# A conditioned two-layer linear attention on one core: weights read by TensorE in two interleaved halves, and row factors turned on VectorE before they go to DRAM

## What is computed

```python
xn = layernorm(x) * scale + bias
q = softmax(xn @ Wq + bq, within a head)
k = softmax(masked(xn @ Wk + bk), over the rows)
v = mask * (xn @ Wv + bv)
att = einsum('bhse,bhsd->bhed', k, v);  y = einsum('bhtd,bhed->bhte', q, att)
h = layernorm(y) * (1 + film_scale) + film_shift
x = x + silu(h) @ W_out + b_out
```

## Time and profile before

| | before |
|---|---|
| median of 3 launches (lowest to highest) | 915.3 us (910.02 to 915.97) |
| the profiled launch, its own time | 911.22 us |
| its span in the profile | 908.9 us |
| TensorE busy | 885.0 us (97%) |
| VectorE, ScalarE, GpSimd busy | 613.2, 398.4, 285.5 us |
| chain that ended last: TensorE, VectorE, DMA | 91%, 4%, 2% of the span |
| chain, rows of L419 on `psum_w` and `psum_k` | 54% and 20% |
| granted TensorE clock, mean | 0.998 |

### The profile page before, as it was taken

One profiled execution on the slowest core, in us unless ns is written; L12 is line 12 of the kernel. 1 busy time (PEld: TensorE's weight loads), 2 busy tenths in 40 slices (PEclk: granted clock), 3 DMA queues, 4 the chain that ended last, 5 costly groups with the idle time before them and its releaser, 6 DMA issues.

```text
span 908.9 us, 15990 instructions
## 1 busy us (share of the span) xinstructions
PE 885.0 (97%) x5883; PEld 736.4 (81%) x5883; DVE 613.2 (67%) x1317; ACT 398.4 (44%) x607; POOL 285.5 (31%) x323
## 2 busy tenths in 40 slices
PE   5999999999999999999999999999999999999998
PEld 4668788887888878788888888888888888888876
DVE  5668676875678677677795775656756575576754
ACT  6226335533444534344553543524345443444433
POOL 2013432404343131433314342132423214243520
PEclk9999999999999999999999999999999999999999
DMA  9672232132312203240130402103030020301202
GB/s 275 234 263 94 64 122 70 34 128 69 138 46 101 107 23 138 69 155 31 65 140 1 151 1 79 60 0 138 0 138 0 20 119 0 138 0 50 90 1 93
DMA packets 30556, 78.31 MB, mean 86 GB/s; under 512 B 11320, under 2 KB 11320, under 8 KB 24640
## 3 DMA queue, kind: packets, MB, share of 16 engines
q1 hardware_dynamic: 30528, 77.93, 23.4%
HBM read 61.12 MB, written 16.80 MB: 86 GB/s over the span
## 4 chain that ended last, share of the span: by engine, by line
PE 91%; DVE 4%; DMA 2%; issue 2%; ACT 1%; POOL 0%; SPq 0%; DVEq 0%; POOLq 0%; ACTq 0%
PE psum_w L419 54%; PE psum_k L419 20%; PE psum_k L659 5%; PE psum_k L626 3%; PE psum_t L649 3%; PE psum_t L492 3%; PE psum_t L479 2%; DMA x_mean_and_rstd<-x_mean_rstd 1%; DVE y L1050 1%; PE psum_t L444 1%; DMA x_in<-in_x 1%; DMA gate<-x_mean_and_rstd 1%; DVE x_in L733 0%; DVE q_rsum L1048 0%; DVE k_exp L965 0%
## 5 line engine op out<-in xcount | busy, mean ns | idle before, releaser
L1253 POOL TENSOR_TENSOR xT_low<-xT,xT_high 128x512 fp32r<-128x512 f32 x60 | 78.4, 1307 | 189.0 <-ACT xT_high L1126 187.7
L976 DVE TENSOR_TENSOR q<-psum_w,bias_q 128x512 f32<-128x512 f32 x64 | 44.3, 692 | 98.7 <-PE psum_w L419 98.7
L419 PE MATMUL psum_k<-w_high_k,xT_high 128*128 128x512 f32 x256 | 104.4, 408 | 4.0 <-DVE y L1050 2.0
L1157 ACT ACTIVATE gate<-psum_t,film_shift,film_scale 128x512 f32<-128x512 f32 x60 | 46.6, 776 | 138.8 <-PE psum_t L492 109.1
L419 PE MATMUL psum_w<-w_high_v,xT_high 128*128 128x512 f32 x256 | 101.3, 396 | 0.0
L419 PE MATMUL psum_k<-w_high_k,xT_low 128*128 128x512 f32 x256 | 100.9, 394 | 0.0
L419 PE MATMUL psum_k<-w_low_k,xT_high 128*128 128x512 f32 x256 | 100.6, 393 | 0.0
L419 PE MATMUL psum_w<-w_high_q,xT_high 128*128 128x512 f32 x256 | 100.1, 391 | 0.0
L419 PE MATMUL psum_w<-w_high_v,xT_low 128*128 128x512 f32 x256 | 99.7, 389 | 0.0
L419 PE MATMUL psum_w<-w_low_v,xT_high 128*128 128x512 f32 x256 | 99.7, 389 | 0.0
L419 PE MATMUL psum_w<-w_high_q,xT_low 128*128 128x512 f32 x256 | 99.6, 389 | 0.0
(11 more groups left out here) (148 smaller groups left out, 1828.6 us busy)
## 6 DMA issues: line engine op xcount, KB each, us to landing
x_in<-x_between_layers SPq DMA_DIRECT2D x9, 1024.0 KB, 4.7
x_res<-in_x SPq DMA_DIRECT2D x8, 1024.0 KB, 6.8
x_between_layers<-x_res SPq DMA_DIRECT2D x8, 1024.0 KB, 3.8
x_in<-in_x SPq DMA_DIRECT2D x7, 1024.0 KB, 4.8
x_res<-x_between_layers SPq DMA_DIRECT2D x7, 1024.0 KB, 6.7
out_x<-x_res SPq DMA_DIRECT2D x7, 1024.0 KB, 3.8
x_in<-in_x_turned SPq DMA_DIRECT2D x6, 1024.0 KB, 5.4
raw_weights<-in_L_cond_film_emb_W SPq DMA_DIRECT2D x4, 1024.0 KB, 7.1
```

The costliest lines, as they stand in the source:

```text
L419: mm = pe.matmul(bank, lhs[:, c, rows_of_tile], rhs[w][:, c, :], start=(c == 0 and n == 0), stop=(c == CHUNKS - 1 and n == 2))
L976: dve.tensor_tensor(q[:, t, :], psum_w[:, t % 2, :], bias_q[:, :], ALU.add)\
L1157: act.activation(gate[:, c % 2, :], psum_t[:, c % 2, :, :].rearrange("p t s -> p (t s)"), ACT.Silu, scale=film_scale[:, cond, c:c + 1].rea ...
L1253: pool.tensor_tensor(xT_low[:, c, :], xT[:, c % 2, :], xT_high[:, c, :], ALU.subtract)\
```

## The change

There are two edits.

The first is on TensorE's reads. On the host, the columns of the eight projection weights are reordered: all even columns first, then all odd ones. On the chip `alternating` reads the row of 512 as two halves of 256 in turns: first of the first half, first of the second, second of the first, and so on. Successive columns of the moving factor are thus 1 KB apart in SBUF, and the product has its columns in the old order. The number and the order of the matmuls stay, and so does everything that is read and written elsewhere.

The second is on the way of the row factors. `x_mean_rstd` becomes 128x32, with the means in columns 0 to 3, the factors in 4 to 7, and zeros behind. `turn_rows` transposes it on VectorE in 32x32 blocks into `x_rows_out`, after the first `q_max` of the iteration. Eight partitions of each of the four blocks then hold 32 neighbouring rows each, and SP stores them with four DMAs of 8 pieces of 128 bytes, where one DMA stored 1024 pieces of 4 bytes.

```diff
-        x_mean_rstd = sb("x_mean_rstd", [P, 2, TILES])
-        x_rstd = x_mean_rstd[:, 1, :]
+        x_mean_rstd = sb("x_mean_rstd", [P, QUAD])
+        x_rstd = x_mean_rstd[:, TILES:2 * TILES]
+        x_rows_out = sb("x_rows_out", [P, QUAD])
...
+        def alternating(w):
+            return w.rearrange("p (a b) -> p b a", a=2)
...
-                sp.wait_ge(x_scale_done, 2 * (i + 1))
-                sp.wait_ge(x_mean_ready, i)
-                sp.dma_start(x_rows.rearrange("n (t p) -> p n t", t=TILES), x_mean_rstd[:, :, :],
-                             allow_slow_non_contiguous=True).then_inc(rows_stored, 16)
-                wait_apart(sp, rows_stored, 16 * (i - 1))
+                sp.wait_ge(x_rows_turned, i - 1)
+                for quad in range(P // QUAD):
+                    sp.dma_start(x_rows.rearrange("n (t a s) -> (n t) a s", t=TILES, s=QUAD)[:, quad, :],
+                                 x_rows_out[quad * QUAD:quad * QUAD + 2 * TILES, :]).then_inc(rows_stored, 16)
+                wait_apart(sp, rows_stored, 16 * (P // QUAD) * (i - 1))
...
-                            mm = pe.matmul(bank, lhs[:, c, rows_of_tile], rhs[w][:, c, :],
+                            mm = pe.matmul(bank, lhs[:, c, rows_of_tile], alternating(rhs[w][:, c, :]),
...
+            def turn_rows(i):
+                dve.wait_ge(x_scale_done, 2 * (i + 1))
+                dve.wait_ge(x_mean_ready, i)
+                dve.transpose(x_rows_out[:, :], x_mean_rstd[:, :]).then_inc(x_rows_turned, 1)
...
+            dve.memset(x_mean_rstd[:, :], 0.0)
...
+                    if t == 0 and host_turned(layer, i):
+                        turn_rows(i + 1)
...
-                    pool.tensor_copy(x_mean_rstd[:, 0, :], x_moments[:, :, 0]).then_inc(x_mean_ready, 1)
+                    pool.tensor_copy(x_mean_rstd[:, 0:TILES], x_moments[:, :, 0]).then_inc(x_mean_ready, 1)
...
+SPLIT_NAMES = [("L0_cond_", "L1_cond_")[layer] + name for layer in range(LAYERS) for name in NAMES[layer].values()]
...
+        if name in SPLIT_NAMES:
+            value = np.asarray(value).reshape(DIM, DIM // 2, 2).transpose(0, 2, 1).reshape(DIM, DIM)
```

More of the change, by code:

```diff
@@ L189, in build_program @@
             sem("x_loaded"), sem("x_stats_done"), sem("x_moments_done"), sem("x_scale_done"), sem("xn_ready"))
-        rows_stored, rows_loaded, x_turned_loaded, x_centred, x_mean_ready = (
-            sem("rows_stored"), sem("rows_loaded"), sem("x_turned_loaded"), sem("x_centred"), sem("x_mean_ready"))
+        rows_stored, rows_loaded, x_turned_loaded, x_centred, x_mean_ready, x_rows_turned = (
+            sem("rows_stored"), sem("rows_loaded"), sem("x_turned_loaded"), sem("x_centred"), sem("x_mean_ready"),
+            sem("x_rows_turned"))
         xT_psum, xT_ready, xT_high_ready, xT_low_ready = (
```

## The result

The changed kernel takes 868.25 us (median of 4 launches, 866.69 to 868.42), the one before 913.5 us (4 launches, 910.02 to 915.97; a fourth launch, 911.71, moved its median from the 915.3 that the prediction starts from). The ratio is 0.9503, with a 95% interval of 0.9465 to 0.9541: 5% faster. The profiled launch took 868.15 us, with a span of 866.0 us.

The account below looks back on a forecast made before the run. TensorE's stream, busy 97% of the span, was taken as the bound. 911.2 - 33 + 3 - 7.6 - 1.5 = 872.1 us for the profiled launch, 876 us as median; 8-in-10 range 865 to 911 us.

Parts of the forecast that it names:

- the excess over columns plus 2.5 ns: TensorE's 3072 projection matmuls: 10.8 ns each, seen only at full clock, go with the new read order; 33 us saved.
- the excess could sit in the stationary factor: Projections: 10.8 ns lie in loading or switching the stationary factor, so read order does nothing; 906 us, chance 0.20.
- The supply gets slower: Projections: columns 1 KB apart may need one read each; up to 1520 us, half-way forms such as 967; chance 0.20.
- each piece read serves again two columns later: TensorE's moving factor: argument against a slower supply, since both streams walk on evenly; no size of its own.
- The store in flight: Layer 0's loop: the 4-byte row-factor store overlaps L626's short TensorE instructions and lengthens them; 7.6 us saved once cleared.
- my 1.4 + 3: SP's row-factor stores: 1.4 us to issue all four, then 3 us until the last lands in DRAM.
- the doubt about pieces below 512 bytes: New row-factor stores: by the Trainium skill's rule, 128-byte pieces would still be slow, but 32 instead of 1024.
- K's wait for y: Layer 0: `gate` lands earlier, so TensorE's 2.0 us of waits for y shrink; 1.5 us saved.
- 3 us given back: Faster projections run into waits for `xT_low` in layer 1 and y in layer 0; 3 us of the saving lost.
- the 4.1 us that I kept: Whole kernel: the median lay 4.1 us above the profiled launch, and the forecast kept that difference.
- edit 2 doesn't clear L626: Layer 0's L626: its excess could belong to the loop, not the store; 884 us, chance 0.10.
- The rival without effect of edit 1: Projections: the order of addresses does nothing, only the new stores gain; 906 us, 903 to 911, chance 0.20.

Follow-up runs that it names:

- step_two: The changed kernel with the moving factor read in steps of two columns (0 2 4 6): 451.3 ns a matmul, 1586.9 us.
- step_four: The changed kernel with the moving factor read in steps of four columns (0 4 8 12): 461.4 ns a matmul, 1617.4 us.
- turns_of_two: The changed kernel with the two halves read two columns at a time in turns (0 1 256 257): 340.2 ns a matmul, 1230.9 us.
- turns_of_four: The changed kernel with the two halves read four columns at a time in turns: 250.0 ns a matmul, 969.6 us.
- The three extra stores: The changed kernel plus one unread store in six iterations, 1024 pieces each: 4 bytes to DRAM 912.0 us, 4 bytes to SBUF 869.3, 128 bytes to DRAM 866.5.

## Why the prediction was right

**The path.** TensorE's stream set the time before and after; its 3072 projections were where the time came from.

**Edit 1, mechanism and size.** The argument was that the excess over columns plus 2.5 ns is a supply that falls short, since half clock hides it, and that the order of addresses acts on it. Forecast 10.8 ns a matmul, 33 us; measured 226.7 - 215.8 = 10.9 ns, 33.5 us. That the excess could sit in the stationary factor is refuted, as nothing was changed there. The order within the row decides, down to 8 or 16 bytes. That what it acts on is a supply stays an inference: the runs show the effect of the order, not its inside. But the argument didn't earn its certainty: of seven other orders one was as fast, one without effect, and five slower. "The supply gets slower", given 0.20 and up to 1520 us, is what step_two (1587) and step_four (1617) did, and a little worse: I had bounded a matmul by half clock's 426.7 ns, and it took 451 and 461. The point in the prediction that kept the loss at a fifth, that each piece read serves again two columns later, was right for this order and doesn't carry: in turns_of_two it holds as well, and that took 340 ns. So the forecast was right on an argument that would have failed for an order next to it, and in this part it had luck.

The Trainium skill's rule on 16-byte lines ("Advanced Engine Details and Errata", section "SBUF Cachelines"), which was the reason for that fifth, has a unit that these runs fit, and a condition that they don't. It promises full performance where accesses that follow each other hit the same line, asks for at least two hits on a line, and names a penalty where each access goes to another line. The change goes to another line with every column and is the fastest (215.8 ns); turns_of_two and turns_of_four have two and four hits in a row and take 340.2 and 250.0. Only step_four, another line with every column and the slowest (461.4 ns), is as the page says. The measurement decides.

**Edit 2, mechanism and size.** The store in flight was named as what lengthens L626, from the overlap of the two. The three extra stores show it. The forecast was 7.6 us; six iterations went from 15.46 us to 6 x 1.30 = 7.8 us, so 7.7. The store lands 2.5 us after its first part was issued, faster than my 1.4 + 3; the doubt about pieces below 512 bytes isn't borne out, even 1024 of 128 bytes land in 2.2 to 2.5 us. The transpose took the 0.20 us taken, and VectorE's wait for `gate` is gone. K's wait for y fell from 2.0 us to 0.7, 1.3 for the 1.5 forecast. But this isn't the new stores' work alone, as the prediction had it: with the stores alone K still waits 1.7 us for y (7 times), so they take off 0.3, and in the changed kernel a wait for `xT_low` of 1.0 us stands beside the 0.7. First with the stores alone, then in the changed kernel:

```profile
PE psum_k L426 <- DVE y L1066: 1.7, 7, 0.3
```

```profile
PE psum_k L426 <- DVE y L1066: 0.7, 3, 0.3
PE psum_k L426 <- POOL xT_low L1269: 1.0, 4, 0.3
```

**The sum.** Of the 911.22 - 868.15 = 43.1 us between the profiled launches, 33.5 + 7.7 + 1.3 = 42.5 are gained and the wait for `xT_low`, which isn't among TensorE's waits before, gives 1.0 back: 41.5. The remaining 1.6 us I can't assign. Two terms were off. "3 us given back" was 1.0. And the 4.1 us that I kept between the profiled launch and the median did not carry over: after, the profiled launch lies at the median. They belong to the kernel before, whose launches scatter (907.4 to 915.97 us). The kernel with the reading in turns alone scatters by 3.5 us; the two with the new stores by 1.7 (the changed kernel) and 0.4 us (stores alone). So the scatter goes with the 4-byte store, though no run was made to show this. These two and what isn't assigned make up nearly all of the difference from 876 to 868.

**What was missed** is that the edits depend on each other. I priced "edit 2 doesn't clear L626" at 884 us, as the forecast without 7.6; the kernel with edit 1 alone took 888.09, since a faster TensorE runs deeper into the store's flight (21.6 us for the six bursts, not 15.5). The rival without effect of edit 1, priced at 906, took 903.0.

## What to carry to other kernels

Where a stream of equal matmuls sets the time, compare the distance of two starts with the columns at the granted clock and with the fixed part that other matmuls show. What is left over may depend on the order in which the moving factor is read, and one try tells; measure it, for neighbouring orders cost from nothing to twice the time. A store of 4-byte pieces to DRAM can be paid by other engines while it is in flight, a burst of short matmuls above all, and not in its own wait row. Look for "issue" gaps that end about when a DMA lands, and turn such values on chip into pieces of 128 bytes first. And price an edit with the others in place: here each was worth some 11 us more beside the other than alone.

## What the runs showed of the hardware that was not expected

- A 512-column fp32r matmul costs 215.8 ns when single columns come from two places 16 bytes or 1 KB apart in turns, 227 ns when they come one after the other, and 250 to 461 ns in five other orders, at a granted clock of 0.997 to 1.0.
- 1024 pieces of 4 bytes to DRAM, 4 KB in all, issued some 3.5 us before a burst of short matmuls, held TensorE for up to 6.3 us at a time, once VectorE for 4.5 us instead, and cost some 45 us in six iterations; the same pieces to SBUF, or 1024 pieces of 128 bytes to DRAM, cost nothing that shows (869.3 and 866.5 us).
- After such gaps the granted clock was lower: 0.67 as a mean from 284.80 to 290.00, behind 5.7 us of idle TensorE. Part of the store's price is paid in the projections behind it.
